# Broadcast rows fetched by DMA and a larger share of drawn rows in the eight-head edge attention of a graph kernel

## What is computed

```
h = (x @ W).reshape(n, heads, out_ch)
a_src = einsum('nhc,hc->nh', h, att_src);  a_dst = einsum('nhc,hc->nh', h, att_dst)
logits = leaky_relu(a_src[src] + a_dst[dst], 0.2)
m = segment_max(logits, dst);  e = exp(logits - m[dst])
denom = segment_sum(e, dst);   alpha = e / denom[dst]
out = segment_sum(h[src] * alpha[:, :, None], dst)
```

## Time and profile before

| | us |
|---|---|
| median of 3 runs | 3289.68 (3289.47 to 3290.33) |
| the profiled execution | 3280.58 |
| its span in the profile | 3278.6 |
| mean granted clock of PE | 0.908 of full |
| POOL's gathers (L1662), from the first to the last | 2379.8 to 2922.0 |
| last join of the eight-head attention ends (L1729) | 2978.45 |

### The profile page before, as it was taken

The page is one execution under the profiler, slowest core; times in us unless marked ns, Lnnn a source line. Parts: engine busy times, 40 slices in busy tenths (PEclk is TensorE's granted clock), DMA queues, the critical chain, the costliest instruction groups (busy, mean ns, idle before and its releaser), DMA issues. The chain is left out here.

```text
span 3278.6 us, 43824 instructions
## 1 busy us (share of the span) xinstructions
PE 2817.9 (86%) x15077; PEld 2124.0 (65%) x15077; DVE 1826.4 (56%) x4185; ACT 1373.2 (42%) x2638; POOL 949.1 (29%) x762
## 2 busy tenths in 40 slices
PE   5778886999996999999999999999876666646997
PEld 3445774677775877878877877886534444444775
DVE  8998657999977541121122112111565565647994
ACT  4574234999995221121111111111341444433897
POOL 6110070000002542213322322221077777750000
PEclk9999897999998999999999999999856666666999
DMA  5334442112002432212211212210211111113200
GB/s 164 136 116 151 186 166 90 41 41 86 1 1 110 186 112 79 76 59 92 91 65 70 91 65 96 91 66 0 77 31 30 29 29 29 29 19 130 81 36 20
DMA packets 73652, 251.60 MB, mean 77 GB/s; under 512 B 20550, under 2 KB 52985, under 8 KB 63737
## 3 DMA queue, kind: packets, MB, share of 16 engines
q1 hardware_dynamic: 57313, 222.42, 18.0%
q0 software_dynamic: 16128, 26.39, 3.7%
HBM read 217.46 MB, written 31.29 MB: 76 GB/s over the span
## 5 line engine op out<-in xcount | busy, mean ns | idle before, releaser
L3095 PE MATMUL psum<-gate_stream,parts 128*128 128x384 f32 (+1 forms) x3600 | 668.0, 344 | 7.5 <-ACT x L3135 4.4
L3095 PEld LDWEIGHTS psum<-gate_stream,parts 128*128 128x128 f32 x3600 | 630.8, 188 | 24.5 <-ACT x L3135 6.0
L3200 POOL CAST gate_stream<-gate_adj 128x1920 fp32r<-128x1920 f16 (+1 forms) x200 | 371.8, 1867 | 834.5 <-PE psum L3095 823.7
L2454 PE MATMUL psum<-gat_h,gat_pair 128*128 128x129 f32 (+1 forms) x3750 | 541.8, 290 | 16.8 <-DVE gat_pair L2258 15.2
L2454 PEld LDWEIGHTS psum<-gat_h,gat_pair 128*128 128x128 f32 (+1 forms) x3750 | 457.6, 191 | 127.8 <-DVE gat_pair L2258 64.9
L3233 DVE SCALAR_TENSOR_TENSOR gate_work<-psum,bhh,gate_work 128x384 f32<-128x384 f32 (+1 forms) x80 | 50.1, 626 | 779.2 <-PE psum L3042 763.2
L1662 POOL DMA_INDIRECT edge_rows<-edge_table,src_idx x416 | 415.8, 999 | 174.3 <-issue 126.5
L2258 DVE SCALAR_TENSOR_TENSOR gat_pair<-gat_above,gat_adj 128x512 f32<-128x512 f32 (+3 forms) x525 | 325.3, 620 | 72.2 <-ACT gat_above L2367 34.7
L2358 ACT ACTIVATE psum<-gat_ad_rows,gat_as 128x512 f32<-128x512 f32 (+3 forms) x525 | 334.9, 638 | 16.9
L2367 ACT ACTIVATE gat_above<-psum,gat_as 128x512 f32<-128x512 f32 (+3 forms) x525 | 324.9, 619 | 39.0 <-PE psum L2442 36.8
L2213 DVE SCALAR_TENSOR_TENSOR gat_acc<-gat_adj,gat_q,gat_acc 128x512 f32<-128x512 f16 (+3 forms) x497 | 327.9, 676 | 0.0
(11 more groups left out here) (508 smaller groups left out, 4088.7 us busy)
## 6 DMA issues: line engine op xcount, KB each, us to landing
gate_adj<-adj SPq DMA_DIRECT2D x35, 2400.0 KB, 8.2
gat_adj<-adj SPq DMA_DIRECT2D x8, 3200.0 KB, 10.5
gcn_adj<-adj SPq DMA_DIRECT2D x10, 2400.0 KB, 8.3
adj<-count_stage SPq DMA_DIRECT2D x196, 100.0 KB, 1.6
gate_adj<-adj SPq DMA_DIRECT2D x5, 2800.0 KB, 9.1
edge_rows<-edge_table,src_idx POOLq DMA_INDIRECT x416, 2.5
gcn_adj<-adj SPq DMA_DIRECT2D x2, 3200.0 KB, 10.3
gcn_adj<-adj SPq DMA_DIRECT2D x2, 2800.0 KB, 9.7
```

The costliest lines, as they stand in the source:

```text
L2454: mm = e.matmul(ps[0:p, b, a:a + D + 1], pair[:, g % 2, i * P:i * P + p], h1[:, hi, h, :], start=hi == 0 and i % 3 == 0, stop=hi == NT - 1 ...
L3095: mm = e.matmul(ps[:, f, 0:hi - lo], parts[:, t, m, f, :], stream[:, (NGG * i + t // GG) % GR, 0:windows(i), t % GG * W:(t % GG + 1) * W], ...
L3200: e.tensor_copy(stream[:, n % GR, 0:windows(i), :], cols[:, i % 2, 0:windows(i), g * GW:(g + 1) * GW]).then_inc(widened, 1)
```

## The change

In words:

- `widen`, `sources`, `lay` and the two tables that they read are gone. SP now fetches each group's places (110 transfers) and each batch's source numbers (13 transfers) from DRAM, 1 KB read once for each of the 128 partitions, into `place_wide`, a ring of 6, and `src_wide`, a ring of 2.
- `hot_t` has three buffers, `product` goes round banks 5, 6 and 7, and an `add` stands two groups behind its `compare`. The offsets of two groups are loaded at once. The filler products of the look-ups are gone.
- `due[c]` = 90 + 5 c: 90 groups before chunk 0, then 5 for each of chunks 1 to 4, none later.
- `DRAWN` = (4, 8, 8, 8, 8, 8, 8, 0): 13 batches in place of 6, 388 gathers in place of 416. With two batches in a chunk's sums, their `pull`s go on consecutive steps, 25 of one, three steps free, 25 of the other. The first `pull` of the second batch waits for the `draw` of the first.
- The joins stand behind L1837, between the `find`s; `ease_off` stands behind the chunk's exponentials.
- The block of tables loses its last two transfers; ahead of it stands a clearing of 24 semaphores.

```diff
-DRAWN = (4, 4, 4, 4, 4, 4, 0, 0)
+DRAWN = (4, 8, 8, 8, 8, 8, 8, 0)
+HEAD = 12
+PRING = 6
+HRING_T = 3
...
-        product = ps[:, 5, 0:EG * 3 * HEADS]
+        product = lambda g: ps[:, 5 + g % 3, 0:EG * 3 * HEADS]
...
-        due = [min(groups, 50 + 12 * c) for c in range(end + 1)]
+        due = [min(groups, 90 + 5 * c) for c in range(end + 1)]
...
+            @block.sync
+            def _(e):
+                def sources(c):
+                    for m in of_chunk[c]:
+                        if m >= 2:
+                            e.wait_ge(ones, (m - 1) * NT)
+                        at = (first_step[c] + batches[m][1]) * P
+                        e.dma_start(src_wide[:, m % 2, :], self.src_scratch[at:at + EG * P].partition_broadcast(P)).then_inc(src_in[m % 2], 16)
+                def places(lo, hi):
+                    for g in range(lo, hi):
+                        if g >= PRING:
+                            e.wait_ge(hots_t, g - PRING + 1)
+                        at = g * EG * P
+                        e.dma_start(place_wide[:, g % PRING, :], self.row_scratch[at:at + EG * P].partition_broadcast(P)).then_inc(
+                            place_in[g % PRING], 16)
+                sources(0)
+                for c in range(end + 1):
+                    places(due[c - 1] if c else 0, due[c])
+                    sources(c + 1)
...
-                    e.wait_ge(wide, g + 1)
-                    if g >= 2:
-                        e.wait_ge(products, g - 1)
-                    e.tensor_scalar(hot_t[:, g % 2, :], ps[:, 6 + g % 2, :], self.pidx[:, 0:1], None,
+                    e.wait_ge(place_in[g % PRING], 16 * (g // PRING) + 16)
+                    if g >= HRING_T:
+                        e.wait_ge(products, g - HRING_T + 1)
+                    e.tensor_scalar(hot_t[:, g % HRING_T, :], place_wide[:, g % PRING, :], self.pidx[:, 0:1], None,
...
-                    for m in of_chunk[c + 1]:
-                        find([(m, 0, NT)])
+                    ahead = of_chunk[c + 1]
+                    if ahead:
+                        find([(ahead[0], 0, HEAD)])
+                    if 0 < c < end:
+                        join_most(c - 1)
+                    if ahead:
+                        find([(ahead[0], HEAD, NT)])
+                    if 0 < c < end:
+                        join_sums(c - 1)
+                    for m, then in zip(ahead, ahead[1:]):
+                        find([(then, 0, HEAD)])
                         draw(m)
+                        find([(then, HEAD, NT)])
+                    if ahead:
+                        draw(ahead[-1])
...
-                    if g:
-                        e.wait_ge(added, g)
-                    e.load(tab_regs, tab_r[0:1, g * EG:(g + 1) * EG])
+                    if g >= 3:
+                        e.wait_ge(added, g - 2)
...
+                            s = 4 + (t + (NT + 3) * i) * (size[c] - 6) // max(slots, size[c] - 6)
+                            pulls_at.setdefault(s, []).append((m, t, t + 1))
```

115 lines of the change are left out of this document (42 added, 73 removed).

## The result

The changed kernel takes **3298.26 us** (median of 19 runs, 3295.53 to 3304.86) where the kernel before, run beside it, takes 3289.57 (19 runs): ratio 1.0031, 95% interval 1.0024 to 1.0038. It is slower by 0.3 per cent; 3260.9 was forecast, and 3298 lies outside the range. The profiled execution took 3295.66, its span 3293.9.

The account below looks back on a forecast made before the run. POOL's gathers were taken to bound the kernel, look-ups nearly as slow. Chunk 2's gathers from 2530.7, four chunks of 73.8, last sums and 61.4 gave 2950.2, 28.3 less; with 0.5 more, 3289.7 - 28.8 = 3260.9 us, range 3252 to 3284.

Parts of the forecast that it names:

- Look-ups, 0.70 per group: Look-ups ahead of chunk 0: 90 groups at 0.70 us each, bounds 0.58 to 0.97, first score at 2472.3.
- the 5.6 us for the packs: Look-ups ahead of chunk 0: 16 packs of 512-column products, half hidden, 0.35 us each, 5.6 us together.
- the sign turns: Look-ups: at 1.02 us per group, a transfer landing of 5.7 us, the change would stop gaining.
- The rival beside that number: Look-ups: SP's place transfers too slow, 1.62 us per group if landing takes 9.3 us, 3344 us; chance 0.08.
- This is the place that decides: End of chunk 0's sums, 2530.7: POOL waits 1.9 us there, and each further microsecond of look-ups counts in full.
- Later chunks, 67.5 us of chain under POOL's 73.8: Chunks 2 to 5: chain of 27.8 + 0.5 + 39.2 = 67.5 us, so POOL sets the pace with 6.3 in hand.
- POOL's 73.8: Chunks 2 to 5: 56 gathers at 1.25 us, 70.0, plus 3.8 for joins, 73.8 us per chunk.
- a pause of 3 us: In the sums: a pause of 3 us could lower the clock, where a pull and step cost about twice 0.56.
- the chain sets the pace: Chunks 1 to 5: rival in which a chunk's chain takes 76 us, not 67.5, giving 3283; chance 0.12.
- The end, 61.4 us: From the end of chunk 5's sums to the last join: 15.0, 14.9 and 31.5, 61.4 us in place of 69.7.
- the most that POOL can give: POOL's gathers: 28 fewer at 1.25 us each, 35 us, as the upper limit of POOL's gain.
- DVE locks POOL out: Rival: 110 compares and 175 additional finds each take 0.35 us from POOL, 100 us, 3361; chance 0.02.

Follow-up runs that it names:

- e1: Changed kernel with the look-ups' register loads left out for all pairs but each chunk's first (wrong tiles read); 0.951 of the kernel before, on a slow chip.
- e9: Changed kernel with the look-ups' register loads left out for all pairs but each chunk's first, on a chip like the first; 3269.3 us, ratio 0.9948.
- e11: Changed kernel with 8 instead of 3 sums between the one-hot products of the first and second four drawn steps; 3281.8 us, ratio 0.9986.
- e12: Changed kernel with the joins back between the scores' steps and ease_off ahead of the exponentials, as in the kernel before; 3324.6 us, ratio 1.0118.
- e7: Changed kernel with the exponentials of chunks 1 to 6 ahead of the one-hots' Relu instead of behind it; 3287.8 us, ratio 1.0002.
- e17: Changed kernel with 72 + 6c look-ups, 8-sum gap, exponentials before Relu, half the one-hots built early, no drawn steps for chunk 6; 3256.3 us, ratio 0.9908.
- e18: Changed kernel with DRAWN (4, 8, 8, 8, 8, 8, 0, 0), so chunk 6's eight steps are POOL's gathers again; 3276.4 us, ratio 0.9971.
- e2: Changed kernel with each look-up group loading its own 4 registers in place of 8 per pair; 0.962 of the kernel before, on a slow chip.
- e4: Changed kernel with 8 instead of 3 sums between the two batches of drawn steps, run on a slow chip; 0.957 of the kernel before.

## Why the prediction was wrong

Its sum put the end of chunk 0's sums at 2530.7, that of chunk 5's at 2888.8, and the last join at 2950.2. Measured: 2550.0, 2924.9, 2986.35. The 36 us between forecast and trace are 19.3 in the first piece, 16.8 in the second and 0.0 in the third. Two of the three pieces were mis-sized, and neither alone would have made the kernel slower: 28.3 us were to be gained.

- **Look-ups, 0.70 per group: the term that failed first.** The gap of 0.39 in the earlier trace rows was taken for the price of one register load, whatever its size, paid once in two groups. It was neither: 0.2 us of that load lay beside the spreading product, which the change removes, and a load grows with its registers (0.33 us for 4, 0.59 for 8). The gap became 0.9 for two groups. The measured 1.02 lies even above the forecast's bound of 0.97, "each group still pays it", though the first score, 20.7 us late, does not: the 5.6 us for the packs were not needed. Score to end of sums took 56.9 us in place of 58.4, so 19.3 remain. 1.02 is also where the prediction said the sign turns, but by this term alone it would not have turned. The rival beside that number named SP's transfers, which is not what happened (e1, e9): transfers allow 0.70.
- **"This is the place that decides"**: right. POOL waits 22.0 us for chunk 0's sums in place of 1.9.
- **Later chunks, 67.5 us of chain under POOL's 73.8: the step that failed second** (16.8 us). The chain was added up as if the multiply were over by the time ScalarE's 27.8 us were. On ScalarE's queue the exponential stands behind the one-hots of its own chunk, so 0.6 us of exponential, 4.42 of multiply and 0.63 up to the first sum come on top, where the forecast had 0.5: 27.7 + 5.7 + 41.4 = 74.8. The cover that was seen to go, 20 us of look-ups, had hidden this order. The sums were 2.2 us longer than the 39.2 forecast, by the low clock behind the stall (e11, e12). That a pause of 3 us could bring the clock down the prediction had said; its argument against, that PE had run through the hand-overs before without a fall, was a misreading: in the kernel before the mean granted clock is 0.57 over 2534 to 2555, behind chunk 0's sums.
- **POOL's 73.8**: near. In e7 and e17, where POOL paces, the scores that wait for gathers are 73 to 76 us apart. The rival "the chain sets the pace" named the right thing at 76 us, with 0.12 for it; its 3283 fell short since it let the look-ups be 0.70.
- **The end, 61.4 us**: measured 61.4. But the step did not ask what the eight drawn steps of chunk 6 buy. The 28 gathers were "the most that POOL can give"; those 8 gave nothing, and their products stood on the path with 20 us (chunk 5's sums, 41.8 us against 22.0 in e18). Without them the change is 0.3 per cent faster than before. That the forecast's end fits to 0.1 us hides this: the 20 us stand in its second piece, in the 39.2 us of chunk 5's sums.
- **DVE locks POOL out**: out, as said. Gathers beside the 175 additional finds take 0.94 us, the mean is 1.008 against 0.999, and joins still make some of 2.3. The Trainium skill's rule on two-port modes ("SBUF — State Buffer", section "Who interferes with whom") is again not what this trace shows for the finds. That a `tensor_tensor` with both inputs in SBUF contends with a GpSimd instruction that reads SBUF, the same section does say, and the prediction left it out; the joins are such instructions, and 1.43 to 2.35 us for the gathers beside them would fit.

## What to carry to other kernels

When a change takes away work that several engines overlapped with, list for each of them what its queue holds between two hand-overs, in its order, and add along that order; an instruction that is ready early but stands behind long ones (here an exponential, 7 us) is part of the chain. Moving work off the pacing engine pays only where that engine is awaited: at the end of a stage look at each chunk by itself. Work that is put ahead of the first hand-over costs its full length for every item, so its price per item has to be known better than anything else. And an idle gap in a profile is what is left of an instruction behind all that ran beside it: before it is used as a price, ask whether what covered it stays.

## What the runs showed of the hardware

- TensorE's register load lasts 0.33 us for 4 and 0.59 us for 8 registers. Products that have been issued run on beside it (0.2 us of the spreading product in the kernel before), but none behind it in the list is issued until it is over: the gap ahead of the look-up products is 0.4 us in the kernel before, 0.6 in e2 with the same load and nothing long beside it, 0.9 with 8 registers.
- On two of the chips the engines stood still between instructions that waited for nothing: in e4 one-hots of 0.40 us follow each other at 1.4 us in places. This is seen only beside POOL's gathers: four of e4's eight rows of one-hots, each with 25 to 32 gathers beside it, have one every 0.51 to 0.65 us on average; one with 14 gathers and the three with none have one every 0.29 to 0.30, as all of e11's do, which is the same kernel on a chip like the first. 334 of the 368 us by which e4's profiled execution is longer than e11's lie in this stage. All kernels took 10 to 16 per cent longer there, the kernel before the most. Timeline of ACT, for e4:

```profile
2749.83 0.40 ACT L1913 ACTIVATE edge_hot<-iota,edge_minus 128x128 f32<-128x128 f32 x1 [0.31 <-issue]
2751.22 0.40 ACT L1913 ACTIVATE edge_hot<-iota,edge_minus 128x128 f32<-128x128 f32 x1 [1.00 <-issue]
2752.62 0.40 ACT L1913 ACTIVATE edge_hot<-iota,edge_minus 128x128 f32<-128x128 f32 x1 [1.00 <-issue]
```

  That the instructions reached the engines late would explain it, but was not shown. The number of instructions alone does not decide: the changed kernel's stage has more of them than that of the kernel before (9214 records in the trace against 8313), and its variants lost less.
- In the sums a pause of 3.3 to 3.4 us of TensorE is followed by a spell at the lower clock, 1.2 GHz, in nearly every chunk: the two zeroing products behind it take 0.90 us, and the sums 41.4 to 41.8. But not always: in e9's chunk 1 the same pause leaves them at 0.54 us and the sums at 38.6; and after e11's 1.86 to 2.08 us they never slow down, while in e17's chunk 4 they do after 2.07. What decides was not tried. Timeline of PE for e9, chunks 1 and 2:

```profile
2575.42 0.54 PE L1963 MATMUL psum<-edge_zero 128*128 128x432 bf16 x2 [3.33 <-DVE edge_rows L1729]
...
2648.86 0.90 PE L1963 MATMUL psum<-edge_zero 128*128 128x432 bf16 x2 [3.32 <-DVE edge_rows L1729]
```
